# A graph convolution's gather queue: stops for its own landings at every second block instead of for the segment sums at every block

## The reference

```python
e0 = feat0[edge_src]; e1 = feat1[edge_src]          # gather of the source node's row
h = gelu(edge_scalar_attr @ W_mlp1 / sqrt(8)); h = gelu(h @ W_mlp2 / sqrt(64))
w00, w01, w10, w11 = h @ Wp_00, h @ Wp_01, h @ Wp_10, h @ Wp_11
out0_a = w00 * e0 * ea0;  out0_b = w11 * sum(e1 * ea1) / sqrt(3)
out1_a = (w01 * e0) x ea1;  out1_b = w10 * e1 * ea0
n0 = segment_sum([out0_a, out0_b], edge_dst); n1 = segment_sum([out1_a, out1_b], edge_dst)
```

## Time and profile before

| | |
|---|---|
| runs | 5021.44, 5057.01, 5386.0 us |
| profiled execution | 5022.96 us, span 5021.2 us |
| TensorE, matmuls | 3679.1 us busy (73%), 13222 instructions |
| VectorE | 1875.9 us (37%) |
| ScalarE | 1335.7 us (27%) |
| POOL | 3166.7 us (63%), of it 3224 gathers of 975 ns |
| mean granted TensorE clock | 0.861 |
| DMA | 254.65 MB, 51 GB/s |

### The profile page before, as it was taken

How to read it: one execution, slowest core, us unless ns; L and a number is a source line. 1 busy time by engine, 2 the same in 40 slices (tenths; PEclk the granted TensorE clock), 3 DMA queues, 4 the chain that set the end, 5 groups by cost and what they waited for, 6 DMA issues and landing times.

```text
span 5021.2 us, 43952 instructions
## 1 busy us (share of the span) xinstructions
PE 3679.1 (73%) x13222; PEld 2590.0 (52%) x13222; DVE 1875.9 (37%) x4551; ACT 1335.7 (27%) x2651; POOL 3166.7 (63%) x3262
## 2 busy tenths in 40 slices
PE   7667777767777777767777777777777677777776
PEld 4445555545555555444555545554555455555555
DVE  4333333333333333333333334333433343334335
ACT  4222222222222222222222222222222222222224
POOL 5656666666666666666666666666666666666660
PEclk8888888888888888888888888898888888888887
DMA  4111111211111121111112111111111111111111
GB/s 162 48 43 48 50 46 48 50 47 47 49 49 48 46 50 48 47 47 46 45 47 50 48 46 50 48 48 49 47 48 50 46 48 50 48 47 47 48 45 57
DMA packets 244371, 254.65 MB, mean 51 GB/s; under 512 B 162332, under 2 KB 188703, under 8 KB 242800
## 3 DMA queue, kind: packets, MB, share of 16 engines
q0 software_dynamic: 103616, 211.52, 16.2%
q1 hardware_dynamic: 139024, 42.54, 3.4%
q10 hardware_dynamic: 1696, 0.18, 0.0%
HBM read 241.18 MB, written 12.80 MB: 51 GB/s over the span
## 4 chain that ended last, share of the span: by engine, by line
another core or an unknown queue 56%; PE 29%; ACT 8%; issue 6%; DVE 1%; ACTq 0%; DMA 0%; DVEq 0%; POOL 0%; POOLq 0%
PE bank L778 9%; PE bank L769 8%; PE bank L764 6%; ACT h L551 3%; PE bank L790 2%; PE bank L798 1%; ACT big L557 1%; ACT idx L536 1%; ACT ztsb L570 1%; ACT dst_rows L566 1%; ACT big L622 1%; ACT dst_rows L565 1%; ACT dst_rows L564 1%; PE bank L723 0%
## 5 line engine op out<-in xcount | busy, mean ns | idle before, releaser
L456 POOL DMA_INDIRECT gath<-feature_table,idx x3224 | 3144.5, 975 | 1733.1 <-issue 1598.8
L769 PE MATMUL bank<-h,w2bd 128*128 128x512 f32 x800 | 580.3, 816 | 1207.2 <-ACT h L551 1150.3
L1042 DVE TENSOR_TENSOR big<-bank,gath 128x256 f32<-128x256 f32 x606 | 254.3, 420 | 2947.8 <-remote 2807.5
L551 ACT ACTIVATE h<-bank 128x512 f32<-128x512 f32 x400 | 238.9, 597 | 3305.3 <-remote 2832.0
L790 PE MATMUL bank<-big,sel 128*128 128x256 f32 x4848 | 1081.3, 379 | 7.3 <-DVE big L1045 7.3
L778 PEld LDWEIGHTS bank<-wpbd,big 128*128 128x128 f32 x3224 | 742.4, 230 | 525.8 <-issue 358.3
L790 PEld LDWEIGHTS bank<-big,sel 128*128 128x128 f32 x4848 | 922.5, 190 | 133.3 <-issue 7.5
L778 PE MATMUL bank<-wpbd,big 128*128 128x256 f32 x3224 | 969.5, 441 | 1.2 <-DVE big L1045 1.2
L769 PEld LDWEIGHTS bank<-h,w2bd 128*128 128x128 f32 x800 | 151.6, 237 | 1379.9 <-ACT h L551 1316.7
L1045 DVE TENSOR_TENSOR big<-bank,gath 128x384 f32<-128x384 f32 x1212 | 613.5, 548 | 0.0
L1032 DVE TENSOR_TENSOR sel<-big,ea_t 128x512 f32<-128x512 bf16 x808 | 527.7, 694 | 0.0
(11 more groups left out here) (90 smaller groups left out, 1431.5 us busy)
## 6 DMA issues: line engine op xcount, KB each, us to landing
gath<-feature_table,idx POOLq DMA_INDIRECT x3224
e<-in_edge_attr SPq DMA_DIRECT2D x204, 64.0 KB
ea_t<-in_edge_attr SPq DMA_DIRECT2D x100, 64.0 KB
feature_table<-gath SPq DMA_DIRECT2D x4, 1280.0 KB, 6.8
out<-big SPq DMA_DIRECT2D x4, 1280.0 KB
big<-in_x SPq DMA_DIRECT2D x3, 1280.0 KB, 10.9
dst_rows<-in_dst SPq DMA_DIRECT2D x1, 1536.0 KB
big<-in_src SPq DMA_DIRECT2D x1, 1280.0 KB
```

The lines of the kernel that those rows point to most:

```text
L456: pool.indirect_dma_start(out=gath[:, s % SLOTS, t, :], out_offset=None, in_=table[:, :], in_offset=bass.IndirectOffsetOnAxis(ap=idx[:, s, ...
L551: act.activation(h1[:, h, :], hid_ps[:, :], ACT.Gelu_apprx_tanh, scale=1.0 / math.sqrt(RADIAL)).then_inc(s_h1[h], 1)
L769: pe.matmul(hid_ps[:, :], w2bd[:, :], h1[:, h, :], start=True, stop=True).then_inc(s_h2p[h], 1)
L1042: dve.tensor_tensor(o[:, :, :, 0, :], w[:, :, :, 0, :], f[:, :, 0, :].unsqueeze(2).to_broadcast([128, n, 2, MUL]), ALU.mult)
```

## The change

POOL no longer waits for the segment sums before a block. From block 6 on, at blocks with an even number only, it waits until the gathers of the last chunk of the block before have landed (`s_g[(s - 1) % SLOTS][3]`); the number of landings is counted by `landed`, the times that slot has been filled. At odd blocks there is neither this wait nor its `sem_inc`. The waits for the indices and for the slot's old rows (L478) and the stops of the first blocks stay as they are, and so do all other engines.

```diff
@@ -468,10 +468,10 @@
 
                 start_stops = {(1, 1): (s_h2p[1], SUPER - 1), (2, 2): (s_rt[1], ROWS), (3, 2): (s_w[1], 1)}
 
-                def gather_block(b, s, free, b_stop, chunks=range(CHUNKS), stops={}):
+                def gather_block(b, s, free, landed, chunks=range(CHUNKS), stops={}):
                     pool.wait_ge(s_idx, b + 1)
-                    if b_stop is not None:
-                        pool.wait_ge(s_seg[CHUNKS - 1], b_stop)
+                    if landed is not None and s % 2 == 0:
+                        pool.wait_ge(s_g[(s - 1) % SLOTS][CHUNKS - 1], landed * (16 * CT))
                         pool.sem_inc(s_round, 1)
                     for c in chunks:
                         if free is not None and c % 2 == 0:
@@ -483,13 +483,15 @@
                         gather(s, c)
 
                 for b in range(RING):
-                    gather_block(b, b, b - SLOTS + 1 if b >= SLOTS else None, b - SLOTS if b > SLOTS else None,
+                    gather_block(b, b, b - SLOTS + 1 if b >= SLOTS else None,
+                                 (b - 1) // SLOTS + 1 if b > SLOTS else None,
                                  stops={c: of for (at, c), of in start_stops.items() if at == b})
                 with pool.Fori(1, ROUNDS) as n:
                     for s in range(RING):
-                        gather_block(n * RING + s, s, n * RING + (s - SLOTS + 1), n * RING + (s - SLOTS))
-                gather_block(BLOCKS - 2, 0, BLOCKS - 2 - SLOTS + 1, BLOCKS - 2 - SLOTS)
-                gather_block(BLOCKS - 1, 1, BLOCKS - 1 - SLOTS + 1, BLOCKS - 1 - SLOTS, range(CUT_C, CHUNKS))
+                        gather_block(n * RING + s, s, n * RING + (s - SLOTS + 1),
+                                     n * (RING // SLOTS) + ((s - 1) // SLOTS + 1))
+                gather_block(BLOCKS - 2, 0, BLOCKS - 2 - SLOTS + 1, (BLOCKS - 3) // SLOTS + 1)
+                gather_block(BLOCKS - 1, 1, BLOCKS - 1 - SLOTS + 1, (BLOCKS - 2) // SLOTS + 1, range(CUT_C, CHUNKS))
             with pool.Else():
                 with pool.Fori(0, BLOCKS) as b:
                     pool.wait_ge(s_idx, b + 1)
```

## The result

The changed kernel is slower: median of four runs 5261.59 us (5228.5 to 5326.46), the kernel before beside it 5176.99 us (5021.44 to 5386.0). The profiled execution took 5285.36 us (span 5283.5); the forecast was 5170 us, in a range of 4800 to 5600. The two profiled executions lie 5.2% apart, since that of before (5022.96 us) was as short as the fastest of the four runs; what follows compares these two.

What follows compares the result with a forecast made beforehand. It took the bound to be TensorE's messages, held until POOL's gathers pause. A pair of blocks goes from 48.1 to 49.6 us, 1.5 us over 98 pairs is +147 us on 5023, so 5170 us, range 4800 to 5600.

Steps and rivals of the forecast that it cites:

- the forecast's own mechanism: POOL halts in the middle of odd blocks, a pair takes 49.6 us against 48.1; given 5060 to 5260 us, chance 0.38.
- What bounds the kernel: Per block: 16 gathers, POOL quiet, TensorE's held messages come out, next 16; 24.06 us each, 48.1 per pair.
- POOL's pattern: POOL per pair: halt for products at an odd block's middle, 8 gathers, landing stop, 24 gathers; 49.6 us.
- gelu to POOL's start: Late-half gelu to POOL's restart: chunk 3's products end after 2.6 us, POOL's next gather 0.85 later; 3.4 us.
- 8 gathers, first to last start: Second half of the odd block on POOL, in steps of 1.28 us, last start at 12.4 us after the gelu.
- landing stop, start to start: New wait at even blocks' heads: landing 2.3 us plus restart 0.85, together 3.2 us where the old stop took 4.7.
- 24 gathers, first to last start: Even block and first half of the odd one on POOL: 23 x 1.28 us, from 15.6 to 45.0.
- last start to the next gelu: TensorE's held messages reach ScalarE 3.8 us (16 gathers) to 5.4 us (32) after the last start; 4.6 for 24.
- ScalarE's cycles: First cycle of a pair ends freely at 19.0 us, the second only once POOL halts, at 49.6.
- The zeros: Costed at zero: waits and increments in POOL's queue while it leads, and the kernel's start and end.
- Rival 1, POOL alone: Faster: messages slip through, pairs go toward POOL's own 42.9 us; 4513 us, or 4768 us halfway; chance 0.27.
- Rival 2, a stop too short: Slower: 3.2 us landing stop falls after 24 gathers and releases nothing; 5709 to 6366 us, mixed form 5461; chance 0.28.

## Why the prediction was right

The sign and the place within the range were right; the median of 5262 us lies 2 us above the 5060 to 5260 that I gave to the forecast's own mechanism. A part of that was luck: the forecast didn't know that there are two kinds of chip. On the second experiment chip the same change took 4444.66 us, outside the range of 4800 to 5600; it was slower there as well, but for the price of the landing stops alone.

**What bounds the kernel: right for the runs it was made from, and wrong as a statement about the kernel.** The loop of 16 gathers, quiet, messages, next 16 was real there, and the changed kernel confirms its reading, since ScalarE's start follows the last gather and not TensorE. But the profile of one chip cannot say that the program brings this about: the same program on three chips has no such loop.

**POOL's pattern: right.** Halts for the products in the middle of odd blocks, eight gathers, a stop, 24 gathers. The forecast's pair and the one shown above, from one late-half gelu to the next:

| step | forecast | measured |
|---|---|---|
| gelu to POOL's start | 3.4 us | 3.36 us (1684.79 to 1688.15) |
| 8 gathers, first to last start | 9.0 | 9.68 |
| landing stop, start to start | 3.2 | 3.57 |
| 24 gathers, first to last start | 29.4 | 29.20 |
| last start to the next gelu | 4.6 | 5.17 |
| pair | 49.6 | 50.98 |

**The terms that were mis-sized** are three. Over the 78 pairs of this pattern the medians of the five steps are 3.27, 9.66, 3.43, 29.31 and 5.06 us, and 50.64 us for the pair. The largest miss, 0.66 us, is the eight gathers. I had taken 1.28 us a step, the mean of a block, but gathers of 1.25 and 1.50 us fall among the first eight after a halt. The trace of before had it: the last of the first eight gathers from 2039.99 on the earlier trace rows starts 9.64 us later,

```profile
2049.63 0.95 POOL L456 DMA_INDIRECT gath<-feature_table,idx  x1 [0.30 <-issue]
```

The second, 0.46 us, is the release after 24 gathers, 5.06 us and not the 4.6 midway between 3.8 and 5.4. The 5.4 was not a good bound: it is the second of the held messages after those 32 gathers, and the first, the early gelu at 2156.00, came 3.9 us after the last start, hardly later than after 16. Why 24 take 5.06 is open. The third, 0.23 us, is the stop. The other two steps were 0.1 us shorter each than forecast. Over the whole loop L475 goes from 197.4 to 5132.3 in 97 pairs, 50.87 us each, against 48.1: 2.8 us times 98 pairs is 271 us, where the two spans differ by 262. The forecast had 1.5 us and 147.

**ScalarE's cycles** were to alternate at 19.0 and 30.6 us; in this pair they are 17.0 and 34.0. The first is shorter than the earlier trace rows made me think, since the end of the loop had other work in it. That doesn't matter for the pair, which POOL's last gather closes.

**The zeros.** I had costed the removed wait itself at nothing because L478 takes its place in the loop. Its 106 waits for the products, 732.9 us in all, show that it did.

**Rival 1, POOL alone,** was false for the forecast's chip and true for the others in one part: there no message is late, and the time is POOL's. By the Trainium skill, SBUF — State Buffer, section "Who interferes with whom", "PE and ACT never wait on anyone". On the three chips that hold nothing the traces agree (no unexplained wait at L551 in 4223 us). On the others 2832.0 us of such waits stand against the rule as the forecast's rival used it; the section itself is about SBUF's ports, and these are waits for a semaphore. The rival had the stops down as pure loss, and the segment sums' stop is none on either kind of chip: without it 1.0006 where nothing is held, and 1.0664 where messages are (there a stop that is met at once stood in its place).

**Rival 2, a stop too short,** was not the case of most pairs: 85 of the 102 stretches of eight end in a landing stop with no first gelu pending, and only ten of the 88 stretches of 24 do. Its mechanism is real: with a stop after each 16 gathers 28 of 45 pending messages came only after POOL's next start. It is not as harsh as I had made it: at nine of those ten stops a message was pending, and it came 3.6 to 5.7 us after the last start, although POOL was already running again.

**What stays open.** What makes one chip hold and another not, or whether it is the chip at all, as none was met twice; whether the loss of records that goes with the hold is its cause, its effect or neither; by which way gathers on POOL hold back TensorE's messages; and whether the effective segment sums' stop at every second block would be slower on a chip that holds, as it was run only on one that doesn't. That the landing stop gives back a part of the loss (1.042 with it, 1.066 where it is met at once) was seen on different chips, and the two intervals overlap.

## What to carry to other kernels

A stop that seems to waste an engine's time can be what lets another engine's messages through: before removing it, look at what the wait behind it (here the products', with four slots) will do, and walk the loop through with it. Take the price of the stop from the distance between starts where the engine is the bound, here 2.2 us for waiting on one's own last gather. And when a stall has no releaser in the profile, run the unchanged kernel on another chip before building on it, and look whether the trace has all its landing records: here 800 us of 5020 were not the program's alone.

## What was not expected of the hardware

- The same program takes 4214 to 4225 us on three chips and 5021 to 5386 us in all runs elsewhere. On the former ScalarE, once free, takes up TensorE's first-layer results within 0.04 us; on the latter those that end after about ten indirect DMAs in a row are taken up a median of 3.8 us (16 in a row) or 5.05 us (24) after the last one's start, if a pause of that length follows. At landing stops after 16 (3.42 us between starts in the median) 28 of 45 came only after the next start. With a pause after every eight, four unexplained waits were left.
- The traces with late messages have 11,419 to 24,206 of the gathers' 51,584 landing records, those without 51,557 or more.
- An indirect DMA of 128 rows of 512 bytes takes POOL 965 ns and one of 64 rows 925 ns, with 0.30 us between any two.
- Nearly four times the packets on SyncE's queue (533,776 against 139,024) changed the time by less than 1% (0.9982, 0.9921 to 1.0042).
